# Macaron layer on one core: the first FFN's last scatter moved wholly into the projections' block, weight split and first products reordered

## What is computed

```python
x = x + 0.5 * ffn(ln(x))        # x: 4096 rows of 256
x = x + attn(ln(x))
x = x + 0.5 * ffn(ln(x))

def ffn(h):                     # 16 experts; each takes 256 tokens of each batch of 2048
    scores = softmax(h @ gate_w.T).transpose(0, 2, 1)
    topk_w, topk_idx = top_k(scores, 256)
    g, u = x_tok @ Wg, x_tok @ Wu            # x_tok: the tokens that an expert chose
    eo = (gelu(g) * u) @ Wd * topk_w
    out = zeros; out[topk_idx] += eo         # scatter with addition
    return out + (gelu(h @ Ws_g.T) * (h @ Ws_u.T)) @ Ws_d.T

def attn(h):                    # 16 heads of 16, causal, rotary positions on q and k
    q, k, v = h @ Wq.T + bq, h @ Wk.T + bk, h @ Wv.T + bv
    ...
```

## Time and profile before

| | |
|---|---|
| median of 3 runs | 1545.61 us |
| profiled execution, its own time | 1542.94 us |
| its span | 1541.2 us |
| PE busy | 1485.7 us, 96% |
| ACT busy | 972.5 us, 63% |
| DVE busy | 902.7 us, 59% |
| POOL busy | 545.9 us, 35% |
| mean granted PE clock | 0.988 |

### The profile page before, as it was taken

How to read it: one execution, slowest core, us unless ns; L and a number is a source line. 1 busy time by engine, 2 the same in 40 slices (tenths; PEclk the granted TensorE clock), 3 DMA queues, 4 the chain that set the end, 5 groups by cost and what they waited for, 6 DMA issues and landing times. The chain is left out here.

```text
span 1541.2 us, 26735 instructions
## 1 busy us (share of the span) xinstructions
PE 1485.7 (96%) x10029; PEld 1046.0 (68%) x10033; DVE 902.7 (59%) x2006; ACT 972.5 (63%) x1322; POOL 545.9 (35%) x474
## 2 busy tenths in 40 slices
PE   4999999999997999999999999999899999999997
PEld 3788888888997873333343343343788888888886
DVE  6788777666655981122145052036787967666663
ACT  7322254444434889999999999998522244445542
POOL 2000256666635971211111021120200045666645
PEclk9999999999998999999999999999899999999999
DMA  8221266666736689505246164122412256666653
GB/s 283 76 67 58 80 181 156 152 148 154 176 70 162 229 262 221 85 3 85 47 90 129 38 116 63 23 70 69 144 55 69 67 157 142 153 157 148 162 111 41
DMA packets 122162, 181.06 MB, mean 117 GB/s; under 512 B 19056, under 2 KB 84080, under 8 KB 119280
## 3 DMA queue, kind: packets, MB, share of 16 engines
q1 hardware_dynamic: 93856, 131.61, 32.3%
q0 software_dynamic: 28176, 47.73, 15.4%
HBM read 123.73 MB, written 55.57 MB: 116 GB/s over the span
## 5 line engine op out<-in xcount | busy, mean ns | idle before, releaser
L2311 ACT ACTIVATE 6418_pr<-6418_pS 128x1024 f32<-128x1024 f32 x448 | 420.3, 1191 | 2.2 <-PE 6418_pS L2221 2.2
L2252 PE MATMUL 6418_pO<-6418_pr,6403_vres 128*32 128x512 f32 x1792 | 237.6, 604 | 0.0
L2221 PEld LDWEIGHTS 6418_pS<-sq_rows,sk_rows 50*128 50x128 f32 x896 | 77.5, 184 | 179.3 <-ACT 6418_pr L2311 132.3
L2221 PE MATMUL 6418_pS<-sq_rows,sk_rows 50*128 50x512 f32 x896 | 183.7, 468 | 2.6 <-issue 1.3
L348 PE MATMUL 15454_pGU<-columns_XT,weights_wts 128*128 128x512 f32 x384 | 152.6, 397 | 0.2 <-DVE 15454_hf L1165 0.2
L998 ACT ACTIVATE hidden_hT<-117_hf 128x512 fp32r<-128x512 f32 x96 | 60.7, 633 | 141.7 <-DVE 117_hf L1165 141.7
L349 PE MATMUL 15454_pGU<-columns_XT,weights_wts 128*128 128x512 f32 x384 | 149.7, 390 | 0.0
L2323 POOL TENSOR_SCALAR_AFFINE_SELECT 6418_pr<-6418_pr 128x512 f32<-128x512 f32 x32 | 20.6, 643 | 364.3 <-ACT 6418_pr L2311 364.3
L350 PE MATMUL 15454_pGU<-columns_XT,weights_wts 128*128 128x512 f32 x384 | 149.6, 390 | 0.0
L998 ACT ACTIVATE hidden_hT<-15454_hf 128x512 fp32r<-128x512 f32 x96 | 60.7, 632 | 139.1 <-DVE 15454_hf L1165 139.1
L1417 POOL DMA_INDIRECT out<-eo,15454_idx x64 | 109.6, 1713 | 98.5 <-issue 67.0
(11 more groups left out here) (416 smaller groups left out, 3568.6 us busy)
## 6 DMA issues: line engine op xcount, KB each, us to landing
117_raw_g<-WgT SPq DMA_DIRECT2D x16, 512.0 KB, 3.9
117_raw_u<-WuT SPq DMA_DIRECT2D x16, 512.0 KB, 3.6
117_raw_d<-WdT SPq DMA_DIRECT2D x16, 512.0 KB, 4.0
q_rows<-rows_halves SPq DMA_DIRECT2D x8, 1024.0 KB, 5.2
k_rows<-rows_halves SPq DMA_DIRECT2D x8, 1024.0 KB, 5.1
15454_raw_g<-WgT SPq DMA_DIRECT2D x16, 512.0 KB, 4.0
15454_raw_u<-WuT SPq DMA_DIRECT2D x16, 512.0 KB, 3.6
15454_raw_d<-WdT SPq DMA_DIRECT2D x16, 512.0 KB, 3.9
```

The costliest lines, as they stand in the source:

```text
L2221: m = t_.matmul(to[:, e, :], key, query, start=True, stop=True)
L2252: m = t_.matmul(pO[e * 32:(e + 1) * 32, j % 2, off:off + wd], vres[:, (g // GB) * TPB + kt, at:at + 32], from_(e), start=n == first[j], st ...
L2311: s_exp.done(a.activation(to, pS[:, u % RING, :, :], ACT.Exp, scale=HD ** -0.5))
```

## The change

Five edits, all at the end of the first FFN and in the first quad of the projections:

1. POOL no longer issues any scatter of the last item in the FFN's block, nor waits there for its results. In the projections' block it issues q = 0 and 1 first of all, then does its three memsets, waits for the landing of both, issues q = 2 and 3, and goes on with `turned(0)`. The memset of `sk` stands behind `turned(0)`.
2. The copy of the projections' weights on ACT goes ahead of chunk 1's steps of the last item (before: behind them), and the subtraction on DVE goes between the two evacuations of the item before the last (before: behind chunk 1's low part).
3. PE turns the first quad column half by column half, not tile by tile, so that the first half's signal comes after four transposes instead of seven.
4. `rows(2)` goes ahead of the turning of quad 1.
5. ACT takes the columns of quad 0 before the deviation of quad 1, and DVE their low parts before the scale of quad 1.

The copy of the row numbers to `last_rows` loses its signal, since the block's end orders it. `scattered` waits for two signals, one for each pair, instead of one.

```diff
@@ -537,7 +537,6 @@
...
 s_wls, s_whs = sig("pool_wl"), sig("pool_wh")
-s_last = sig("dve_last_rows")
 s_Dq, s_evq = sig("pe_last_D"), sig("dve_last_ev")
@@ -1047,15 +1046,15 @@
...
         hidden(s, 0)
-        hidden(s, 1)
-        if lead and s == NI - 2:
-            split(s, 2)
-            split(s + 1, 0)
         if lead and s == NI:
...
             s_wh.done(a.activation(self.lead_w[0][:, :, :], self.qkv_raw[:, :, :], ACT.Copy))
+        hidden(s, 1)
+        if lead and s == NI - 2:
+            split(s, 2)
+            split(s + 1, 0)
         if J - 3 <= s < J:
@@ -1246,6 +1245,10 @@
...
             evacuate(s, 0)
+            self.counter("proj_w", 16).wait(v, 2)
+            s_wh.wait(v, 3 * (E + 1) + 1)
+            s_wl.done(v.tensor_tensor(self.lead_w[1][:, :, :], self.qkv_raw[:, :, :], self.lead_w[0][:, :, :].bitcast(f32),
+                                      ALU.subtract))
             evacuate(s, 1)
@@ -1253,11 +1256,6 @@
...
         low(s, 1)
-        if s == NI:
-            self.counter("proj_w", 16).wait(v, 2)
-            s_wh.wait(v, 3 * (E + 1) + 1)
-            s_wl.done(v.tensor_tensor(self.lead_w[1][:, :, :], self.qkv_raw[:, :, :], self.lead_w[0][:, :, :].bitcast(f32),
-                                      ALU.subtract))
         if s == NI - 2:
@@ -1351,7 +1349,7 @@
...
         v.wait_ge(*s_idx.at(1))
-        s_last.done(v.tensor_copy(self.last_rows[:, :, :], idx[:, E - 2:E, 1, :]))
+        v.tensor_copy(self.last_rows[:, :, :], idx[:, E - 2:E, 1, :])
     for s in range(J + 1, NI + 2):
@@ -1398,13 +1396,8 @@
...
         else:
-            s_sc[1 - k].wait(g, (e - 1) // 2 + 1 - (0.5 if lead and item == NI - 1 else 0))
-        if lead and item == NI - 1:
-            s_last.wait(g, 1)
+            s_sc[1 - k].wait(g, (e - 1) // 2 + 1)
         for q in range(4):
-            if lead and item == NI - 1 and q == 2:
-                g.wait_ge(*s_evq.at(4))
-                return
             if lead and item == NI - 3 and q == 2:
@@ -1413,8 +1406,7 @@
...
                 self.settle(g)
-            where = self.last_rows[:, q // 2, q % 2:q % 2 + 1] if lead and item == NI - 1 else place_of(item, q)
-            sent = g.indirect_dma_start(out, bass.IndirectOffsetOnAxis(where, 0), eo[:, k, q, :],
+            sent = g.indirect_dma_start(out, bass.IndirectOffsetOnAxis(place_of(item, q), 0), eo[:, k, q, :],
                                         None, compute_op=ALU.add)
@@ -1458,7 +1450,7 @@
...
             gather(J + 1)
-    for s in range(J + 1, NI + 2):
+    for s in range(J + 1, NI + 1 if lead else NI + 2):
         if J + 1 < s + 1 < NI and s > J:
@@ -1510,12 +1502,12 @@
...
 s_sent = [sig(f"scattered{k}", 64) for k in range(2)]
-s_late = sig("proj_scattered", 32)
+s_late = [sig(f"proj_scattered{e}", 32) for e in range(2)]
 
...
         eng.wait_ge(*s_sent[k].at(0))
-    eng.wait_ge(*s_late.at(1))
+        eng.wait_ge(*s_late[k].at(1))
 
@@ -1627,11 +1619,10 @@
...
 
-    for j in range(4):
-        for c in range(DC):
+    for c in range(DC):
+        for j in range(4):
             m = t_.transpose(pX[:, c, j * P:(j + 1) * P], self.lead_x[0][:, j, c * P:(c + 1) * P], self.ident[:, :])
-            if j == 3:
-                s_T.done(m)
+        s_T.done(m)
     t_.wait_ge(*s_set.at(2))
@@ -1641,9 +1632,12 @@
...
             norms(q - 1)
+        else:
+            rows(2)
         if q + 1 < J:
             turn(q + 1)
-        rows(4 * q + 2)
+        if q >= 1:
+            rows(4 * q + 2)
         rows(4 * q + 3)
@@ -1696,8 +1690,8 @@
...
     s_xn.bump(a)
+    columns(0)
     deviation(1)
-    columns(0)
     normalize(1)
@@ -1779,8 +1773,8 @@
...
     statistics(1)
+    low_columns(0)
     scale(1)
-    low_columns(0)
     for q in range(J):
@@ -1821,17 +1815,22 @@
...
 def on_gpsimd(g):
+
+    def scatter(e):
+        self.settle(g)
+        for q in (2 * e, 2 * e + 1):
+            s_late[e].part(g.indirect_dma_start(x, bass.IndirectOffsetOnAxis(self.last_rows[:, e, q % 2:q % 2 + 1], 0),
+                                                self.eo[:, 1, q, :], None, compute_op=ALU.add), 16)
+
+    for k in range(2):
+        g.wait_ge(*s_sent[k].at(0))
+    scatter(0)
     s_clear.done(g.memset(zero[:, :], 0.0))
...
     s_clear.done(g.memset(heads[:, :, :, HD:HD + 1], 1.0))
-    g.wait_ge(*s_sent[1].at(0))
-    self.settle(g)
-    for q in range(2, 4):
-        s_late.part(g.indirect_dma_start(x, bass.IndirectOffsetOnAxis(self.last_rows[:, q // 2, q % 2:q % 2 + 1], 0),
-                                         self.eo[:, 1, q, :], None, compute_op=ALU.add), 16)
-    g.wait_ge(*s_xn.at(2))
-    s_clear.done(g.memset(self.sk[:, 0, :, :].bitcast(f32), 1.0))
+    g.wait_ge(*s_late[0].at(1))
+    scatter(1)
 
@@ -1847,6 +1846,9 @@
...
         turned(n)
+        if n == 0:
+            g.wait_ge(*s_xn.at(2))
+            s_clear.done(g.memset(self.sk[:, 0, :, :].bitcast(f32), 1.0))
         if 1 <= n <= POOL_LOW:
...
         return {"sync": on_sync, "tensor": on_tensor, "scalar": on_scalar, "vector": on_vector, "gpsimd": on_gpsimd}
```

## The result

The changed kernel takes 1549.55 us (median of 20 runs, 1545.98 to 1551.69). The kernel before, run beside it, takes 1546.3 (20 runs): a ratio of 1.0019, with a 95% interval of 1.0013 to 1.0025, or 2.9 us more by the ratio (3.25 between the two medians). The forecast was 2.7 us less.

What follows compares the result with a forecast made beforehand. All engines wait for POOL at the FFN block's end, then POOL's pairs gate DVE's rotations. The block starts 6.45 us earlier, but POOL's scatters leave rotation 8 2.7 us earlier: 1545.61 - 2.7 = 1542.9, range 1539.2 to 1546.6.

Steps and rivals of the forecast that it cites:

- T: Start of the projections' block, forecast at 478.65 instead of 485.1, 6.45 us earlier, with POOL's drain no longer ending last.
- The split: Earlier weight subtraction on DVE, 1.76 us, hidden in a 1.90 us idle gap; PE's last FFN product 0.9 us earlier.
- The landing: First scatter pair in the projections' block landed at T + 9.1 = 487.8; bounds 484.4 to 489.7 (T + 1.9 + 9.2).
- The nearest case: Worst scatter landing on line 1417, 7.3 us, issued just ahead of SP's loads; taken as the first scatter's travel time.
- the row of 9.2: Landing time of the line 1831 scatter pair under SP's block-start loads, 9.2 us; used for the latest bound, 489.7.
- From rotation 4 to rotation 8 DVE needs 511.0 - 500.93 = 10.1 us: DVE's unchanged time in the projections; the second pair's landing would take over only if later than 498.2.
- The second pair's landing: DVE's wait before rotation 4: landing between 494.3 and 499.6, taken as 495; decides only if later than 498.2.
- one of the prediction's signs of being wrong: In the projections: rotation 4 waiting on the scatters rather than rotation 8 on POOL.
- ACT's wait for POOL: ACT's high half of pair 0 waits for POOL until 494.8, holding the squares; forecast well ahead of the earlier 502.2.
- The slower one: Rival: scatters wait behind SP's loads, POOL behind them; decides if the first pair lands after T + 11.9; chance 0.12.
- the two slower rivals: Scatters behind SP's loads, 2.7 us slower, 1548.3, chance 0.12; block's end staying late, 3.4 us slower, 1549.0, chance 0.05.
- the freely travelling scatters: Rival: first pair lands at 484.4 as without traffic, rotation 8 6.1 us earlier, 1539.5; chance 0.25.

Runs made afterwards that it cites:

- e3: The change with DVE's shift written as four one-input operations instead of one with two inputs; ratio 0.9995 to the kernel before.
- e11: The change with one more wait: POOL waits for its own memset of sk to complete before pair 1; ratio 0.9999 to the kernel before.
- e5: The change with the edits of e3 and e4 together; ratio 0.9984 to the kernel before.
- e2: The kernel before with the scatters' move alone, split and products in the old order; ratio 1.0025 to the kernel before.
- e4: The change with POOL's memset of sk put ahead of the wait for the first pair's landing; ratio 1.0000 to the kernel before.
- e8: The change with SP's loads behind load(2) held until the first pair of scatters has landed; ratio 0.9971 to the kernel before.
- e12: e8 with POOL also waiting for its own memset of sk before pair 1; ratio 0.9963 to the kernel before.
- e7: e5 with SP's loads behind load(2) held until the first pair of scatters has landed; ratio 0.9974 to the kernel before.
- e1: The change with the scatters' move undone, the earlier split and the reordering kept; ratio 0.9980 to the kernel before.

## Why the prediction was wrong

- **T: right.** 6.45 us earlier was forecast, 6.35 came. PE's idle time at the block's start is 0.38 us, its granted clock is 1.00 over 487 to 489, the upper level of 2.4 GHz, and PE's wait of 0.97 is gone. The split fits where it was put: the second evacuation now waits 0.24 us instead of 1.90.
- **The landing: mis-sized.** "The first pair has landed at T + 7.3 + 1.8 = T + 9.1" was off by 2.4 us, and T + 11.5 lies past the latest bound too (T + 11.1): POOL's third scatter started at T + 12.3, not T + 9.9. I took POOL's first issue to be at T; it came 0.7 us later, and the scatters took nearly as long beside SP's loads as the late ones of before. The nearest case, taken from the FFN's block, was the wrong one; the row of 9.2 was right (8.5 and 8.9 now). Pair 0 came at T + 15.2 (T + 13.6), 15.9 us of POOL's work up to the end of pair 1 took 16.1, and in e3 rotation 8 duly followed POOL's pair 1: at +47.3, 0.9 us earlier than before, where 2.7 were forecast. So the wrong size took 1.8 us of the gain of 2.7; the 0.9 left are too few to show in e3's ratio (0.9995, 0.9986 to 1.0004).
- **"From rotation 4 to rotation 8 DVE needs 511.0 - 500.93 = 10.1 us": the step that failed.** It took 17.4. This interval held a shift of 1.13 us, and I took its row over as the price of the operation. It was the price of the operation beside POOL as POOL worked then. With the scatters directly ahead of pair 0 the same operation took 5.63 us, 4.5 more, against a forecast gain of 2.7. By e3 and e11 it is what made the change slower: +108.4 and +109.2 without the hold, +114.5 with it, and ratios of 0.9995 and 0.9999 for 1.0019. The hold cost the 0.2%, and the late landing most of what was to be won.
- **The second pair's landing** was forecast at 495, with 498.2 as the point from which it decides. It came at 498.4, which is 496.8 counted as before, 3.9 us behind its last issue: late because it was issued late. Rotation 4 waited 4.55 us for it, one of the prediction's signs of being wrong, and in e3 this still left the gate to POOL.
- **ACT's wait for POOL** was named ("pair 0 now waits for POOL until 494.8"), but it lasted until 498.64, or 497.0 counted as before, 2.2 us longer than said. PE waited 5.2 us, and its clock was 0.73 over 500 to 510. In e3 PE still waits 4.7 us for the squares and its clock is 0.90 over 500 to 510, with the exponential at +108.4, so this wait is not what made the change slower.
- **The rivals.** The slower one named late scatters, and they were late, but at T + 11.5 they stayed short of the point from which it decides (11.9). The mechanism that decided was none of the four. That the times of the two slower rivals, 1548.3 and 1549.0, lie near the 1549.55 measured is chance.

The Trainium skill, "SBUF — State Buffer", section "Who interferes with whom", says that the ports which VectorE and GpSimd share are an exclusive lock: a VectorE instruction with two SBUF inputs contends with a GpSimd instruction that reads SBUF, and who comes second is blocked while the other's instruction lasts; a VectorE instruction with at most one SBUF input, outside the modes that use two ports, doesn't contend. I had not weighed it. The traces agree with the kind: 0.58 us with one input, in e3, beside POOL's overlapping work; and in before and in e11 the end together with one POOL operation. By the same rule the hold in the change would have been the rest of the operation under way, an estimate of 0.8 us from its row (503.88 + 2.97 = 506.85, against 506.03). Here it passed over three more (506.22, 507.48, 508.72) and took 5.63, and the measurement decides.

The rule of the Trainium skill that the prediction set against rows 9 ("DMA: Bandwidth & Descriptors", section "Queues, rings and completion order": each DMA engine round-robins between its queues) gave the freely travelling scatters. They did not travel freely: in e5 no scatter packet moved in the first 4 us. But once they moved they had a share, 129 packets beside 277 of SP's queue from 488 to 490, so they did not wait for all of the loads either.

## What to carry to other kernels

A duration in a timeline is the price of an operation beside what its neighbours did at that time: where a change makes GpSimd work in another rhythm, look for VectorE operations with two SBUF inputs beside it, however small. In these traces the sign was GpSimd rows that last clearly longer than the distance of their starts (1.86 us at 1.25), behind a scatter: count such an operation as held to GpSimd's next stop. One wait of GpSimd for its own result ended it here, for 0.7 us. And a transfer issued by GpSimd at the start of a block competes with the loads that SyncE issues there: hold those that aren't needed yet, and look at which later transfer they then meet (here the second pair).

## What the runs showed of the hardware that was not expected

- One VectorE operation on 128x4 elements took 5.63, 5.63, 4.31 and 3.60 us (the change, e2, e4, e8), each time to the end of GpSimd's last operation before a pause; 1.13, 0.84 and 0.35 us (before, e11, e12), each time to the end of the one operation under way, where GpSimd's operations did not overlap.
- GpSimd's rows come in two kinds, 1.29 and 1.86 us for the same operation at the same distance of 1.25 us. In these traces the second kind begins behind an indirect DMA issue that a memset or an addition follows at once, and lasts until GpSimd waits.
- Scatters issued at T + 0.7, ahead of most of SyncE's loads, moved their first packets 4 to 5 us later (e5); with the loads held it was 2 to 3 us, and they had landed at T + 6.4 (e7), against T + 11.5 in the change.
- GpSimd's drain at the block's end lasted until the scatter under way had landed and 0.9 us more (5.73 us, to 484.8, with a landing at 480.07 + 3.8 = 483.9; 5.91 us in e1); with the scatters moved it was over at 477.4, before PE's at 480.0.
